# Graph kernel on one core: the table stage in another order, with q's copies shared and nine places for x

## What is computed

```
h = x
for l in range(3):                      # three layers
    agg = segment_sum(h[src], dst)
    z   = (1 + eps[l]) * h + agg
    h   = relu(z @ W1[l] + b1[l]) @ W2[l] + b2[l]
x1 = layernorm(x + h)
hij = concat(x1[src], x1[dst])
e   = leaky_relu(hij @ w, 0.2) @ a
att = exp(e) / segment_sum(exp(e), src)[src]
out = layernorm(x1 + segment_sum(x1[src] * att, dst))
```

## Time and profile before

| | us |
|---|---|
| median of 3 runs | 9425.27 (9423.82 to 9440.45) |
| the profiled execution | 9423.8 |
| its span, first to last instruction | 9421.9 |
| busy: PE, DVE, ACT, POOL | 6930.8, 5344.6, 4915.2, 7019.2 |

### The profile page before, as it was taken

One profiled execution on the slowest core, in us unless ns is written; L12 is line 12 of the kernel. 1 busy time (PEld: TensorE's weight loads), 2 busy tenths in 40 slices (PEclk: granted clock), 3 DMA queues, 4 the chain that ended last, 5 costly groups with the idle time before them and its releaser, 6 DMA issues.

```text
span 9421.9 us, 148124 instructions
## 1 busy us (share of the span) xinstructions
PE 6930.8 (74%) x27727; PEld 4811.7 (51%) x27728; DVE 5344.6 (57%) x18202; ACT 4915.2 (52%) x11010; POOL 7019.2 (74%) x7500
## 2 busy tenths in 40 slices
PE   5777777777777777777777777777777777777786
PEld 3444444444444444444444444566666676666665
DVE  4444444444444444444444444567777777778888
ACT  5555555556555555555555555422222222267777
POOL 5777777767777777767777777667777777778886
PEclk7666666676666666676666666788888878789988
DMA  3222222232222222222222222366666666655454
GB/s 91 53 53 53 53 53 53 53 77 53 53 53 53 53 53 53 53 75 53 53 53 53 53 53 53 90 174 182 181 183 181 183 181 182 182 136 140 139 140 133
DMA packets 937711, 898.45 MB, mean 95 GB/s; under 512 B 258861, under 2 KB 778726, under 8 KB 937635
## 3 DMA queue, kind: packets, MB, share of 16 engines
q0 software_dynamic: 244544, 529.59, 21.9%
q1 hardware_dynamic: 627697, 265.87, 10.1%
q10 hardware_dynamic: 65426, 102.51, 4.0%
HBM read 751.91 MB, written 143.82 MB: 95 GB/s over the span
## 4 chain that ended last, share of the span: by engine, by line
POOL 62%; issue 23%; DVE 7%; PE 3%; ACT 2%; DVEq 1%; POOLq 1%; DMA 1%; ACTq 0%; SPq 0%
POOL rows L753 54%; POOL work L753 6%; DVE agg L1547 4%; POOL hot L753 2%; DVE big L1781 2%; ACT hot L1032 1%; PE psum L1288 1%; PE psum L1163 1%; PE psum L1177 1%; POOLq L765 0%; ACT work L1069 0%; POOLq L458 0%; DMA big<-in_dst 0%; DVEq L1781 0%; PE psum L1186 0%
## 5 line engine op out<-in xcount | busy, mean ns | idle before, releaser
L1155 PE MATMUL psum<-work,rows 128*128 128x256 f32 x9408 | 4290.9, 605 | 1522.3 <-DMA rows<-table_g,idx_now 998.7
L1561 DVE TENSOR_TENSOR agg<-agg,psum 128x128 f32 x9408 | 2704.3, 287 | 3135.2 <-PE psum L1155 2821.4
L1155 PEld LDWEIGHTS psum<-work,rows 128*128 128x128 f32 x9408 | 2494.7, 292 | 3317.4 <-issue 1215.0
L753 POOL DMA_INDIRECT rows<-table_g,idx_now x3136 | 2961.7, 944 | 1021.7 <-issue 1021.1
L917 ACT ACTIVATE work<-big,one_col 128x1024 f32<-128x1024 f32 x1176 | 1348.1, 1147 | 2350.7 <-PE psum L1155 2347.6
L909 ACT ACTIVATE big<-iota_w,rel_now 128x256 f32<-128x256 f32 x4704 | 1971.6, 495 | 51.9
L753 POOL DMA_INDIRECT rows<-in_x,idx_now x1568 | 1479.8, 944 | 533.2 <-issue 532.8
L993 ACT ACTIVATE work<-psum 128x256 f32<-128x256 f32 x832 | 320.6, 385 | 1453.6 <-PE psum L1253 1448.3
L753 POOL DMA_INDIRECT rows<-table_p,idx_now x832 | 801.8, 964 | 265.7 <-issue 263.9
L1288 PE MATMUL psum<-rows,hot 128*128 128x128 f32 x3328 | 659.4, 326 | 227.3 <-ACT hot L1032 200.5
L1249 PE MATMUL psum<-big,work 128*128 x3328 | 777.6, 321 | 47.4 <-ACT work L994 31.3
(11 more groups left out here) (196 smaller groups left out, 5447.8 us busy)
## 6 DMA issues: line engine op xcount, KB each, us to landing
rows<-x_of SPq DMA_DIRECT2D x416, 256.0 KB, 2.9
work<-rel_rows ACTq DMA_DIRECT2D x208, 256.0 KB, 3.8
x_of<-rows SPq DMA_DIRECT2D x208, 256.0 KB, 4.2
rows<-table_g,idx_now POOLq DMA_INDIRECT x3136
x_of<-work SPq DMA_DIRECT2D x156, 256.0 KB
big<-lo_rows ACTq DMA_DIRECT2D x208, 192.0 KB, 3.2
rows<-in_x,idx_now POOLq DMA_INDIRECT x1568
rows<-table_p,idx_now POOLq DMA_INDIRECT x832
```

The lines of the kernel that those rows point to most:

```text
L753: pool.indirect_dma_start(out=to, out_offset=None, in_=table, in_offset=bass.IndirectOffsetOnAxis(ap=idx_now[:, at:at + 1], axis=0)) \
L1155: ins = pe.matmul(sums_at(q, t % QUAD), ring[:, t, :], span_hot[q][:, t % QUAD, :], start=True, stop=True)
L1561: dve.tensor_tensor(to, to, sums_at(q, j)[:, k * P:(k + 1) * P], ALU.add).then_inc(added[a], 1)
```

## The change

VectorE's iteration k now takes y and the moments of block k, and then the reciprocal and x1 of block k - 1; before, the reciprocal and x1 of block k itself. It copies Q only for even blocks; ScalarE copies Q of the odd ones after P's copy. A new semaphore `q_kept` counts those, and TensorE and the end of the loop wait for both. The loop's iterations of GpSimd, SP (but for the distance of the loads) and TensorE keep their order. `x_in` has nine places and lies where `g_rows` was, so SP first waits for the last table stores and then loads nine blocks ahead of the third layer.

```diff
@@ SP
             def load_x(b):
+                if b >= X_BUFS:
+                    sp.wait_ge(x_loaded[b % 3], 16 * len(range(b % 3, b, 3)))
                 for p, c, rows_of_x in x_rows(x, b):
-                    sp.dma_start(x_in[p, b % 3, c, :], rows_of_x).then_inc(x_loaded[b % 3], 16)
+                    sp.dma_start(x_in[p, b % X_BUFS, c, :], rows_of_x).then_inc(x_loaded[b % 3], 16)
...
-            for b in range(3):
+            for s in range(G_BUFS):
+                sp.wait_ge(table_out[s], 16 * (LAYERS - 1) * len(range(s, BLOCKS, G_BUFS)))
+            for b in range(X_BUFS):
                 load_x(b)
             stage_ahead(2)
...
             for k in range(BLOCKS + 2):
-                if k + 3 < BLOCKS:
+                if k + X_BUFS < BLOCKS:
                     sp.wait_ge(y_done, k + 1)
-                    load_x(k + 3)
+                    load_x(k + X_BUFS)
@@ GpSimd
                 if k < BLOCKS:
-                    s = k % 3
-                    pool.wait_ge(x_loaded[s], 16 * sum(x_parts(b) for b in range(s, k + 1, 3)))
+                    s, at = k % 3, k % X_BUFS
+                    known = max(k + 1, X_BUFS)
+                    pool.wait_ge(x_loaded[s], 16 * sum(x_parts(b) for b in range(s, known, 3)))
                     n = n_chunks(k)
-                    pool.tensor_tensor(x_in[:, s, 0:n, :], x_in[:, s, 0:n, :],
+                    pool.tensor_tensor(x_in[:, at, 0:n, :], x_in[:, at, 0:n, :],
@@ ScalarE
                     act.activation(p_rows[:, b % 3, 0:n, 0:PW], psum[:, 4:4 + n, 0:PW], ACT.Copy).then_inc(p_taken, 1)
+                    if b % 2:
+                        act.activation(q_block(b), psum[:, 4:4 + n, PW:2 * PW], ACT.Copy).then_inc(q_kept, 1)
@@ TensorE
                         pe.wait_ge(p_taken, b)
-                        pe.wait_ge(q_taken, b)
+                        pe.wait_ge(q_taken, (b + 1) // 2)
+                        pe.wait_ge(q_kept, b // 2)
@@ VectorE
                     dve.wait_ge(x_biased, k + 1)
-                    dve.tensor_tensor(y[:, s, 0:n, :], by_chunk(ps[1 + 2 * s][:, 0:n * D], n), x_in[:, k % 3, 0:n, :],
+                    if k >= 2:
+                        dve.wait_ge(x1_done, k - 1)
+                    dve.tensor_tensor(y[:, s, 0:n, :], by_chunk(ps[1 + 2 * s][:, 0:n * D], n), x_in[:, k % X_BUFS, 0:n, :],
                                       ALU.add).then_inc(y_done, 1)
                     moments(y_done, k + 1, lambda c: y[:, s, c, :], k, n)
-                    inverse(k, k % 3, n)
-                    if k >= 3:
-
-                        dve.wait_ge(p_stored[k % 3], 16 * (k // 3))
-                        dve.wait_ge(x1_kept, k - 2)
+                if 1 <= k <= BLOCKS:
+                    b = k - 1
+                    s, n = b % 3, n_chunks(b)
+                    inverse(b, s, n)
+                    if b >= 3:
+
+                        dve.wait_ge(p_stored[s], 16 * (b // 3))
+                        dve.wait_ge(x1_kept, b - 2)
                     for c in range(n):
-                        ins = dve.tensor_scalar(p_rows[:, k % 3, c, PW:ROW], y[:, s, c, :], mean_var[:, k % 3, c, 0:1],
-                                                rstd[:, k % 3, c:c + 1], ALU.subtract, ALU.mult)
+                        ins = dve.tensor_scalar(p_rows[:, s, c, PW:ROW], y[:, b % 2, c, :], mean_var[:, s, c, 0:1],
+                                                rstd[:, s, c:c + 1], ALU.subtract, ALU.mult)
                     ins.then_inc(x1_done, 1)
-                if k >= 2:
+                if k >= 2 and k % 2 == 0:
```

More of the change, by code:

```diff
@@ L73 @@
 G_BUFS = 4
+X_BUFS = 9
 X_BANKS = (5, 6, 7)
@@ L224, in gnn @@
         g_rows = work[:, 0:G_BUFS * W].rearrange("p (s c d) -> p s c d", s=G_BUFS, c=C)
-        y = work[:, 6 * W:8 * W].rearrange("p (s c d) -> p s c d", s=2, c=C)
-        x_in = work[:, 8 * W:11 * W].rearrange("p (s c d) -> p s c d", s=3, c=C)
+        x_in = work[:, 0:X_BUFS * W].rearrange("p (s c d) -> p s c d", s=X_BUFS, c=C)
+        y = work[:, X_BUFS * W:11 * W].rearrange("p (s c d) -> p s c d", s=2, c=C)
         x1_t = work[:, 11 * W:13 * W].rearrange("p (s w) -> p s w", s=2)
@@ L407, in gnn @@
         q_taken = sem("q_taken")
+        q_kept = sem("q_kept")
         p_stored = sems("p_stored", 3)
@@ L491, in x_rows, with q_block @@
                     (slice(0, N_LAST), slice(C_LAST - 1, C_LAST), ap[n1:N, :].rearrange("(c p) d -> p c d", c=1))]
+        def q_block(b):
+            n = n_chunks(b)
+            return q_rows[:, b * C * PW:(b * C + n) * PW].rearrange("p (c f) -> p c f", c=n)
         def table_block(table, b):
@@ L1226, in _ @@
             pe.wait_ge(p_taken, BLOCKS)
-            pe.wait_ge(q_taken, BLOCKS)
+            pe.wait_ge(q_taken, (BLOCKS + 1) // 2)
+            pe.wait_ge(q_kept, BLOCKS // 2)
             def add_den(i, q):
@@ L1650, in _ @@
                     dve.wait_ge(p_taken, b + 1)
-                    dve.tensor_copy(q_rows[:, b * C * PW:(b * C + n) * PW].rearrange("p (c f) -> p c f", c=n),
-                                    psum[:, 4:4 + n, PW:2 * PW]).then_inc(q_taken, 1)
+                    dve.tensor_copy(q_block(b), psum[:, 4:4 + n, PW:2 * PW]).then_inc(q_taken, 1)
             def wide(col, n):
@@ L1720, in score_turn @@
                         hot_pairs(i + 1, k - QUADS // 2)
-            dve.wait_ge(q_taken, BLOCKS)
+            dve.wait_ge(q_taken, (BLOCKS + 1) // 2)
+            dve.wait_ge(q_kept, BLOCKS // 2)
             dve.wait_ge(x1_kept, BLOCKS)
```

## The result

The changed kernel takes 9465.93 us (median of 5 runs, 9463.20 to 9483.42), the kernel before 9424.45 us in the same series: ratio 1.0047, interval 1.0036 to 1.0057. It is 41 us slower; 18.3 were forecast, and the time lies above the range.

The account below looks back on a forecast made before the run. VectorE's own order was taken to bound the table stage, becoming an open round trip through GpSimd; 18.3 us added to the median 9425.27 gave 9443.6 us, range 9436 to 9458.

Parts of the forecast that it names:

- The period: Table stage, y to y of successive blocks: 5.16 us against 4.30 before, 0.86 more per block; chance 0.75.
- y to x1's end: VectorE's part of a table stage block, from y to the end of the last x1: 3.225 us.
- GpSimd's leg: Table stage, x1's end through GpSimd's copy and bias add to the next y: 1.935 us, the longer leg.
- TensorE's: Table stage, TensorE's leg from x1's end through transposes and down to y: 1.60 us, lower bound of period 4.83.
- 0.7 + 21 x 0.86 - 0.5 = 18.3 us: Table stage: late start 0.7, 21 blocks each 0.86 longer, shorter bias add of last block 0.5 less.
- goes into the total one to one: Table stage, 112 us or 1.2% of the span: the next gathers start after it, so its length counts fully.
- Half of q's copies: Table stage: moving them to ScalarE saves VectorE 0.30 us a block on the mean; ScalarE has cover enough.
- The saving: Rival, table stage: VectorE's own order stays the bound at 3.5 us a block, -16.8 us, 9408.5; chance 0.04.
- GpSimd's leg didn't get shorter: Rival, table stage: beside an idle VectorE GpSimd's leg shortens, TensorE's bounds at 4.83, 11.3 us more, 9436.6; chance 0.06.
- TensorE kept the 2.4 GHz level: Rival, table stage: TensorE loses its clock; a third of blocks at 1.2 GHz gives 9456, all 9482; chance 0.10.
- The burst of x loads: Rival, third layer's start: nine loads hold up the gathers, up to 14 us more, 9458; chance 0.05; taken as 0.
- The condition that I named for being wrong: Whole kernel: the prediction is wrong if the table stage's length explains less than nine tenths of the difference.

Follow-up runs that it names:

- e1: The changed kernel run once more with a profile of its own, against the kernel before: 9463.39 us against 9423.14, ratio 1.0045.
- e8: The changed kernel with 12 idle memsets on VectorE ahead of the table stage and GpSimd copying one block later, against the kernel before: ratio 1.0011.
- e13: The changed kernel with 12 idle memsets on VectorE ahead of the table stage, more rounds, against the kernel before: 9442.08 us against 9423.16, ratio 1.0022.
- e4: The kernel before with only half of q's copies moved to ScalarE, against the kernel before: 9441.48 us against 9423.14, ratio 1.0019.
- e5: The kernel before with half of q's copies on ScalarE and 12 idle VectorE memsets ahead of the table stage: 11156.22 us against 11163.24, ratio 0.9994.
- e9: The changed kernel with 12 idle memsets on VectorE ahead of the table stage, against the kernel before, on a chip with longer gather stages: ratio 1.0025.
- e7: The changed kernel with 12 idle VectorE memsets, GpSimd copying one block later and TensorE running down one block earlier, against the kernel before: ratio 0.9996.
- e2: The kernel before with only the nine places for x and their loads, against the kernel before: 9423.72 us against 9423.14, ratio 1.0000.
- e3: The kernel before with only VectorE's new order, against the kernel before: 9442.32 us against 9423.14, ratio 1.0022.
- e6: The kernel before with 4 idle memsets on VectorE ahead of the table stage, against the kernel before: ratio 0.9995.

## Why the prediction was wrong

**The table stage was right.** The period is 5.22 us (e1: y(2) at 6051.96, y(3) at 6057.17), forecast 5.16. The terms: y to x1's end 3.22 (forecast 3.225), GpSimd's leg 2.00 (1.935). Of the latter the step from the bias add's end to y was too small: 6097.57 + 1.27 to 6098.93 are 0.09 us; I had taken 0.03 from a single row of the kernel's start. Over 22 blocks that is 1.3 us. y(2) and y(3) were forecast at 6052.1 and 6057.3. GpSimd's leg, not TensorE's, sets the period, and TensorE's measures 1.63 once the other is gone (e8). The stage grew by 19.4 us against 18.3, and the change without its displacement costs 18.9 us (e13).

**The step that failed** is the sum, "0.7 + 21 x 0.86 - 0.5 = 18.3 us", as the whole difference. The stage's length "goes into the total one to one", and of everything outside it the prediction weighed only the start of the third layer; the last edge stage was put at nothing without a reason. It grew by 21.3 us. Half of q's copies was priced in the table stage alone, and there the reading held: ScalarE had the cover, and the copies cost nothing (e4 is even 2.7 us shorter). But taking 12 instructions out of VectorE's program moved VectorE's last loop, and this cost 21 us, 0.21 in each of 102 turns; put back as idle memsets, they give it back (e5, e9). It is a term of its own, larger than all the others. No row of the table stage could have shown it. The trace of the kernel before shows that this loop waits at its head 101 times, 22.8 us in all; that this depends on the place of the loop no run had shown before e5. Why the place matters stays open.

**The rivals.** The saving didn't arrive, as the untouched orders of TensorE and GpSimd said; e7, which changes both orders, shows that they held it back. GpSimd's leg didn't get shorter beside an idle VectorE: the add takes 1.27 as before. TensorE kept the 2.4 GHz level from 6056 on at 56 to 69% busy, with 1.87 us idle in a block of 5.22 (the prediction has 1.4, but its own terms give 5.16 - 3.48 = 1.68), as the stretch of the earlier trace rows had let expect; it fell only at the stage's end, behind 6176:

```profile
6050.00:6056.00 6.00, 5.20 (x25) 4.40 (x24) 3.81 (x15) 2.08 (x5) 1.70 (x3) 0.72 0.15 44
6056.00:6062.00 6.00, 4.13 (x29) 3.56 (x28) 3.12 (x14) 2.92 (x6) 2.62 (x3) 1.00 0.57 192
...
6116.00:6122.00 6.00, 3.35 (x20) 2.78 (x20) 4.43 (x22) 2.06 (x5) 1.84 (x2) 1.00 0.46 143
```

(columns as in the earlier trace rows, e1). The first profile has one dip, to 0.67 from 6081 to 6086; its y still start 5.22 us apart there. The burst of x loads cost nothing: in e1 the gathers of the third layer start at 4075.08, in the kernel before at 4075.09, and e2's time is that of the kernel before.

**The range** was built from bounds of the table stage and of the layer's start alone. The condition that I named for being wrong, the stage's own length explaining less than nine tenths of the difference, is what happened: it explains half.

## What to carry to other kernels

When a producer is moved later in one engine's order, walk the other engines' orders for the next thing that it waits for: work that two engines had done in the cover of a whole iteration became a serial leg, and the larger of the two set the period. Moving the consumers' steps by one block as well (e7) turned 137 us into 110. And a loop that is bound by one engine's own order can change its time when instructions are added or removed ahead of it in that engine's program, as this one did: compare the stages that the change doesn't touch, and put fillers in before a small difference is put down to the change itself.

## What the runs showed of the hardware

The last edge stage takes 1070, 1085, 1091 or 1094 us with the same loop on VectorE, by how many instructions stand ahead of it (0 and +4, +20, -12, +52). The differences sit in two waits of VectorE, in e1 both in the half behind the loop's jump back: 0.23 to 0.36 us in front of the loop's first instruction, and 119 to 130 us in all in front of the instruction behind the load of window numbers. It was the same on four chips (e3 1070.0, e6 1069.6, e9 1070.2, e13 1070.1 at place 0 or +4).

The Trainium skill, Runtime: NRT & Kernel Launch, section Instruction fetch mechanics, says that instructions are fetched in sequence, in blocks of 256, and that a taken branch whose target isn't in the two blocks at hand has to wait for its block. The runs agree in part: one of the two waits is at the jump and depends on the place. But it grows by only 0.10 to 0.14 us a turn, the other wait, which grows by as much at -12 and +52, isn't at the jump, and with -12 and +20 slow and 0 and +4 fast between them it is no single border of a block that the loop crosses. No run here tells whether the fetch is the cause.
